# The T half of a triangular inverse kept in its PSUM bank, in a fused delta-rule attention and mixture kernel

## The reference, cut to what matters

```python
def step(S, inp):
    qt, kt, vt, gt, bt = inp
    S = S * jnp.exp(gt)[..., None]
    err = jnp.einsum('bhk,bhkv->bhv', kt, S)
    delta = bt[..., None] * (vt - err)
    S = S + kt[..., None] * delta[:, :, None, :]
    ot = jnp.einsum('bhk,bhkv->bhv', qt, S)
    return (S, ot)
```

## Time and profile before

| | us |
|---|---|
| median of 3 runs | 5753.49 (5748.64 to 5756.43) |
| the profiled execution, its own time | 5752.94 |
| its span | 5751.1 |
| PE busy | 5436.6 (95%) |
| DVE busy | 4370.1 (76%) |
| ACT busy | 3026.7 (53%) |
| POOL busy | 1729.5 (30%) |

### The profile page before, as it was taken

The page is one execution under the profiler, slowest core; times in us unless marked ns, Lnnn a source line. Parts: engine busy times, 40 slices in busy tenths (PEclk is TensorE's granted clock), DMA queues, the critical chain, the costliest instruction groups (busy, mean ns, idle before and its releaser), DMA issues. The chain is left out here.

```text
span 5751.1 us, 87343 instructions
## 1 busy us (share of the span) xinstructions
PE 5436.6 (95%) x28996; PEld 3760.2 (65%) x28996; DVE 4370.1 (76%) x9309; ACT 3026.7 (53%) x5708; POOL 1729.5 (30%) x1766
## 2 busy tenths in 40 slices
PE   5599999999999999999999999999999999799999
PEld 2277777777777777777777777777777777444444
DVE  6688888888888888888888888888888888121110
ACT  3366666666666666666666666666666665100110
POOL 2233333333333333333333333333333333000000
PEclk8799999999999999999999999999999999899999
DMA  2111111111111111111111111111111110331221
GB/s 77 47 28 38 30 38 30 36 30 36 30 35 30 37 30 38 30 38 30 38 30 38 30 34 34 30 38 30 37 30 38 30 30 19 106 112 51 71 75 50
DMA packets 192038, 235.69 MB, mean 41 GB/s; under 512 B 41576, under 2 KB 136424, under 8 KB 187504
## 3 DMA queue, kind: packets, MB, share of 16 engines
q1 hardware_dynamic: 111016, 188.22, 10.9%
q10 hardware_dynamic: 80584, 41.95, 2.5%
HBM read 183.75 MB, written 46.38 MB: 40 GB/s over the span
## 5 line engine op out<-in xcount | busy, mean ns | idle before, releaser
L713 PE MATMUL bank<-xT,weights 128*128 128x512 f32 x4096 | 2128.4, 607 | 32.9 <-PEq L155 32.9
L1451 POOL TENSOR_TENSOR KR<-KR,decay_u 128x256 f32<-128x256 f32 x768 | 635.3, 827 | 1599.1 <-PE bank L733 1591.1
L733 PEld LDWEIGHTS bank<-KQ,KR 128*128 128x128 f32 x7168 | 915.3, 191 | 267.9 <-issue 241.6
L1035 DVE TENSOR_TENSOR KQ<-KQ,decay_u 128x512 f32<-128x512 f32 x896 | 789.5, 881 | 284.3 <-PE bank L733 279.2
L733 PE MATMUL bank<-KQ,KR 128*128 128x128 f32 x7168 | 963.3, 277 | 18.2 <-DVE KQ L1035 17.3
L1020 DVE SCALAR_TENSOR_TENSOR conv<-pre,taps,conv 128x512 f32<-128x512 f32 x1152 | 938.5, 815 | 18.2 <-ACT conv L1243 8.5
L1051 DVE COPY_PREDICATED all_pairs<-level_mask,bank 128x256 f32<-128x256 int32 x1792 | 822.4, 523 | 0.0
L713 PEld LDWEIGHTS bank<-xT,weights 128*128 128x128 f32 x4096 | 664.4, 192 | 186.5 <-issue 164.5
L757 PEld LDWEIGHTS bank<-T_inv,pairs 128*128 128x128 f32 x1536 | 270.9, 190 | 566.1 <-ACT T_inv L1308 326.0
L757 PE MATMUL bank<-T_inv,pairs 128*128 128x128 f32 x1536 | 495.6, 407 | 113.1 <-ACT T_inv L1308 112.9
L1308 ACT ACTIVATE T_inv<-bank 128x256 fp32r<-128x256 f32 x640 | 247.1, 386 | 479.6 <-PE bank L775 476.4
(11 more groups left out here) (185 smaller groups left out, 8805.7 us busy)
## 6 DMA issues: line engine op xcount, KB each, us to landing
decay_u<-decay_scratch SPq DMA_DIRECT2D x128, 510.0 KB
beta_u<-beta_scratch SPq DMA_DIRECT2D x128, 256.0 KB
y_in<-y_scratch SPq DMA_DIRECT2D x32, 1024.0 KB, 4.8
y_scratch<-y_rn ACTq DMA_DIRECT2D x112, 256.0 KB, 2.3
xt<-in_L_attn_hidden_states SPq DMA_DIRECT2D x8, 1024.0 KB, 5.4
x_in<-in_L_attn_hidden_states SPq DMA_DIRECT2D x28, 256.0 KB, 5.0
out<-o_out ACTq DMA_DIRECT2D x28, 256.0 KB, 2.0
w<-in_L_ffn_W SPq DMA_DIRECT2D x8, 704.0 KB, 4.8
```

The source lines that it names most:

```text
L713: last = nc.tensor.matmul(bank[w % 2][:], weights[par][:, w, k, :], xT[:, k, u % J * UC:(u % J + 1) * UC], start=k == 0, stop=k == KC - 1)
L733: last = nc.tensor.matmul(to[:, :, i], KR[:, cols(i)], second if i < COUPLES else second[:, :, ::-1, ::-1], start=True, stop=True)
L1035: nc.vector.tensor_tensor(second_halves, second_halves, pair[:, :, 0:1].unsqueeze(1).to_broadcast([P, 2, blocks, 1 << l]), ALU.mult).then_ ...
L1451: nc.gpsimd.tensor_tensor(firsts, firsts, second.to_broadcast([P, 2, UC >> (l + 2), 1 << l]), ALU.mult).then_inc(keys_scaled.sem, 1)
```

## The change

T of the inverse is no longer rewritten from a fresh product at each level. It stays in PSUM bank 5, and each level adds to it: one matmul for each couple, with a gathered weight tile XX (POOL copies the parts of X into it, three copies for a level) and a plain copy of Z as the moving operand (ACT, `keep_z`, five more copies). So `inverse_xt(l)` splits into `inverse_t(l)`, two matmuls of 128 columns for levels 1 to 5, and `inverse_x(l)`, two matmuls. The first T comes from the first X by two matmuls of 256 columns with a swap matrix, and ACT copies it (`take_t(m, 0)`), so `first_inverse` on DVE goes. Z moves from bank 5 to the upper half of bank 2, beside X. The pair products are in natural order, so `keep_pairs` copies with one instruction instead of two, and ACT turns the kept pairs with three copies instead of one. The blocks of X are stored with the turned sequences first. The lists of calls on PE, ACT, DVE and POOL are rearranged.

```diff
@@ PE: the first T, Z, T and X
-            def transpose_pairs():
-                wait(pe, pairs_ready, m, 1)
-                for i in range(B):
-                    last = nc.tensor.matmul(bank[5][:, cols(i)], pairs_first[:, cols(i)], ident_r[:], start=True, stop=True)
+            def first_t():
+                wait(pe, x1_ready, m, 1)
+                for turned in range(2):
+                    last = nc.tensor.matmul(bank[5][:, to], swap_r[:], swapped, start=turned == 0, stop=turned == 1, ...)
             def inverse_z(l):
-                if l == 1:
-                    wait(pe, t1_ready, b, 1)
-                else:
-                    wait(pe, t_ready, b, l - 1)
+                wait(pe, t_ready, b, l)
+                if l >= 2:
+                    wait(pe, x_ready, b, l - 1)
-            def inverse_xt(l):
+            def inverse_t(l):
+                wait(pe, z_kept, b, l)
+                wait(pe, xx_ready, b, l)
+                for r in range(COUPLES):
+                    last = nc.tensor.matmul(firsts_in_place(bank[5], l, r), XX[:, cols(r)], Z[:, cols(r)],
+                                            start=False, stop=True, skip_group_check=True)
+                last.then_inc(t_done.sem, 1)
+            def inverse_x(l):
-                if l < LEVELS - 1:
-                    for i in range(B):
-                        last = nc.tensor.matmul(bank[5][:, half_cols(i)], X[b % 2][:, cols(i)],
-                                                halves(ZI[:, cols(i % COUPLES)], l, i // COUPLES), start=True, stop=True)
@@ DVE
             def add_identity_to_z(l):
-                wait(dve, z_done, b, l)
+                if l < LEVELS - 1:
+                    wait(dve, z_kept, b, l)
+                else:
+                    wait(dve, z_done, b, l)
-            first_inverse()
@@ ACT
+            def keep_z(l):
+                wait(act, z_done, b, l)
+                nc.scalar.activation(Z[:], bank[2][:, UC // 2:UC], ACT.Copy).then_inc(z_kept.sem, 1)
             silu_v()
-            take_t(1)
+            keep_z(1)
+            store_output()
+            take_t(b, 1)
             take_x(1)
-            store_output()
+            keep_z(2)
             take_projection(2)
...
+            take_t(m, 0)
             take_projection(1)
@@ POOL
+        def gather_x(u, l, before):
+            wait_apart(pool, x_ready.sem, x_ready.at(u, l - 1), pool_waits_passed)
+            wait_apart(pool, t_done.sem, t_done.at(u, l), pool_waits_passed)
...
+            nc.gpsimd.tensor_copy(halves(XX[:], l, 1), halves(natural, l, 1).bitcast(F32))
+            for i in range(COUPLES, B):
+                last = nc.gpsimd.tensor_copy(halves(XX[:, cols(couple(i))], l, 0),
+                                             halves(X[u % 2][:, cols(in_x(i))], l, 0).bitcast(F32))
+            last.then_inc(xx_ready.sem, 1)
```

More of the change, by code:

```diff
@@ L579, in attention, with couple, sides, all_first_sides @@
     COUPLES = B // 2
-    def in_order(ap, i):
-        return ap if i < COUPLES else ap[:, ::-1]
-    def first_sides(tile, l, r):
+    def couple(i):
+        return min(i, B - 1 - i)
+    def sides(tile, l, first, step, start, blocks):
+        size = 1 << l
+        ap = tile[:]
+        return bass.AP(tensor=ap.tensor, offset=ap.offset + first * P + start,
+                       ap=[list(ap.ap[0]), [step * P + size - 2 * start, 2], [2 * size, blocks], [1, size]])
+    def first_sides(tile, l, r):
+        return sides(tile, l, r, B - 1 - 2 * r, 0, P >> (l + 1))
+    def all_first_sides(tile, l):
+        return sides(tile, l, 0, COUPLES, 0, COUPLES * P >> (l + 1))
+    def in_x(i):
+        return (i + COUPLES) % B
+    def x_second_sides(tile, l, r):
+        size = 1 << l
+        natural, turned = in_x(r) * P + size, in_x(B - 1 - r) * P
+        ap = tile[:]
+        return bass.AP(tensor=ap.tensor, offset=ap.offset + natural,
+                       ap=[list(ap.ap[0]), [turned - natural, 2], [2 * size, P // (2 * size)], [1, size]])
+    def all_x_second_sides(tile, l):
+        return sides(tile, l, 0, COUPLES, 0, COUPLES * P >> (l + 1))
+    def firsts_in_place(tile, l, r):
         size = 1 << l
@@ L800, in apply_inverse @@
                 for i in range(B):
-                    last = nc.tensor.matmul(bank[7][:, cols(i)], X[u % 2][:, cols(i)], to[:, cols(i)], start=True, stop=True)
+                    last = nc.tensor.matmul(bank[7][:, cols(i)], X[u % 2][:, cols(in_x(i))], to[:, cols(i)], start=True, stop=True)
                 return last
@@ L913, in step @@
             level(0)
-            inverse_xt(1)
+            inverse_t(1)
             refine(c, 1)
+            inverse_x(1)
+            inverse_z(2)
             project(2, (3,))
-            inverse_z(2)
             level(1)
+            inverse_t(2)
+            correct_by_residual(1)
+            inverse_x(2)
             project(3, (0,))
-            inverse_xt(2)
-            correct_by_residual(1)
+            inverse_z(3)
             project(3, (1,))
-            inverse_z(3)
+            level(2)
+            inverse_t(3)
+            output()
+            inverse_x(3)
+            inverse_z(4)
             project(3, (2,))
-            level(2)
-            inverse_xt(3)
-            output()
+            level(3)
+            inverse_t(4)
+            next_state()
+            inverse_x(4)
             project(3, (3,))
-            inverse_z(4)
-            next_state()
-            level(3)
-            inverse_xt(4)
+            inverse_z(5)
             project(0, (0,))
-            inverse_z(5)
+            level(4)
+            inverse_t(5)
+            right_side()
+            inverse_x(5)
             project(0, (1,))
-            level(4)
-            inverse_xt(5)
+            inverse_z(6)
             project(0, (2,))
-            inverse_z(6)
-            right_side()
             level(5)
-            inverse_xt(6)
+            inverse_x(6)
             project(0, (3,))
@@ L1475, in step @@
                 squares_left(s.a, 1)
+                for l in range(2, LEVELS - 1):
+                    gather_x(s.b, l, None)
                 return
```

150 lines of the change are left out of this document (87 added, 63 removed).

## The result

The changed kernel takes 6727.15 us, median of 4 runs (6722.37 to 6728.86), beside 5751.07 for the kernel before (also 4 runs). The ratio is 1.1692, 95% interval [1.1678, 1.1706]. The forecast was 6360 us with a range to 6530: the direction held, the size did not. The profiled execution took 6722.37 us, its span is 6720.6.

The account below looks back on a forecast made before the run. The prediction took PE to bound the kernel, busy 35.28 of a 36.14 us step. It added 3.9 of lateness and 1.0 of low clock, 4.9 us over about 124 steps, 608 us on 5752.9: 6360 us, range 6080 to 6530.

Parts of the forecast that it names:

- the main term: Level 1 T and X copies queue behind ACT's output store; PE waits 3.1 us at `inverse_z(2)`, `level(1)` ends 3.85 late.
- PE stays the bound: Rival: with y_rn early enough PE sees only its lighter work, 2.2 us a step less, 5480 us; faster, chance 0.06.
- the idle: PE's waits in a step: 1.3 us at `inverse_t(1)`, 3.1 at `inverse_z(2)`, 0.6 at `inverse_z(4)`, 1.7 at `right_side`.
- the clock term: PE's clock falls to half rate after the new idle; 3.4 us at half rate costs up to 1.7, taken as 1.0.
- the sum of 3.9: `level(5)` and all after it late by 1.75 at `right_side` plus 2.16 of work formerly done earlier: 3.9 us a step.
- DVE's chain to the state: From `scale(1)` to the new state on DVE, 13.4 us, nearly all busy; starting at 2133.3, state at about 2146.9.
- `right_side`: PE waits 1.7 us there for DVE's state and starts 1.75 us later than before.
- the small edits: POOL's three gathers at most 1.5 us and hidden; `first_inverse` goes where DVE idles anyway; reversed operands cost nothing.
- the 1.3 us of PE's work: PE's saving a step from fewer T matmuls: 1.1 us on five levels and 0.2 on the first T.
- the clock falls in every step and the gathers collide: Rival: 3.9 + 1.7 + 0.5 = 6.1 us a step, 6510 us; chance 0.14.
- DVE is not last at `right_side`: Rival: only PE's own lateness counts, 2.7 us a step without a clock fall, 335 us, 6090; chance 0.14.

Follow-up runs that it names:

- The store's edit: Changed kernel with the store of the output moved behind the copies of T and X of level 1 on ACT: 6268.67 us, ratio 1.0897.
- the same swap in the old kernel: Kernel before, with its store of the output put ahead of the copies of T and X of level 1 on ACT: 5936.3 us, ratio 1.0313.
- The fillers: Changed kernel with five unread 512-column matmuls a step in PE's three idle gaps, no wait removed: 6352.78 us, ratio 1.1043.
- The experiment that moved it: Changed kernel with `right_side` put back behind Z of level 6 and two quarters of the projection on PE: 6665.6 us, ratio 1.1584.
- all orders mended: Changed kernel with store and `right_side` late, ACT's Z, T, X copies ahead of work waiting for DVE, Z of levels 2 and 4 behind a projection quarter: 5666.24 us, 0.9847.
- both edits: Changed kernel with the store behind T and X of level 1 and `right_side` behind Z of level 6: 6269.16 us, ratio 1.0898.
- T and X of level 5 moved too: Changed kernel with store and `right_side` late, plus ACT's copies of T and X of level 5 ahead of `silu_squares(1)`: 5932.54 us, ratio 1.0317.

## Why the prediction was right, and where it failed

**Right: the chain.** The step called the main term, T and X behind the store, is there as forecast: from `scale(0)` to the store 2.89 us (2948.75 to 2951.64) where 2.88 was taken, and 2.83 of wait where 3.1 was taken. The store's edit alone gave back 458 us, and the same swap in the old kernel cost 181. What the rival "PE stays the bound" needed, an early y_rn, did not arise.

**Right in size, in part by luck: the idle.** 6.73 us of waits in the step shown, against 6.7 forecast. The two waits at the head are each 0.3 shorter than forecast as the rows count them, and the one for the state 0.66 longer, so misses cancel in the sum.

**Failed, first and most: the clock term.** The prediction took 1.0 us a step, with "a stretch of 3.4 us at half rate costs up to 1.7" as the bound. The fillers measure 2.93. The step that failed is the count of stretches: the bound priced one of 3.4 us in a step, as the earlier trace rows show after one wait. Two waits, 0.97 and 2.83 with 1.6 us of work between them, go with 6.83 us at half rate (81 such stretches in 91 steps), and a further stretch of 3.41 comes in about every second step, mostly behind the 2.36 of `right_side`: 7.8 us in the mean. The conversion was right in kind, about 0.38 us lost for each us at half rate (2.93 / 7.8). It is under the half, and some of the slow time is spent waiting: 0.90 of the 6.83 in the step shown. The 1.93 missing are 245 us of the 367 by which the forecast was low.

**Failed, second: the sum of 3.9.** At full clock the step is 4.64 longer, 0.74 more than forecast, 94 us. (The other 28 of the 367 are 3 more steps than the 124 counted, and the time outside the steps.) Most of it comes out at `right_side`, which waited 2.36 and not 1.7. The term that was mis-sized is DVE's chain to the state. The walk put 13.6 us from the start of `scale(1)` to the new state on DVE. In the kernel with all gaps filled it takes 14.44 (2980.91 to 2995.35):

```profile
2980.91 0.70 DVE L1089 TENSOR_TENSOR KQ<-KQ,decay_u 128x512 f32<-128x512 f32 x1 [0.32 <-PE bank L758]
...
2987.43 0.42 DVE L1134 TENSOR_TENSOR ZI<-bank,ident_each 128x256 fp32r<-128x256 f32 x1 [0.32 <-ACT Z L1362]
...
2992.07 0.42 DVE L1134 TENSOR_TENSOR ZI<-bank,ident_each 128x256 fp32r<-128x256 f32 x1 [0.92 <-ACT Z L1362]
...
2994.24 1.11 DVE L1171 SCALAR_TENSOR_TENSOR state<-state,chunk_decay,bank 128x128 f32<-128x128 f32 x4
```

I had counted this chain as nearly all busy. In the kernel before it is, with one wait of 0.20:

```profile
2141.37 0.42 DVE L1079 TENSOR_TENSOR ZI<-bank,ident_each 128x256 fp32r<-128x256 f32 x1 [0.20 <-PE bank L757]
```

Now DVE idles in it 0.32 for Z of level 4 and 0.92 for Z of level 5, which ACT has to copy first, and another 0.32 just ahead of `scale(1)`. `keep_z` lies between PE and DVE on levels 1 to 5; I had priced that only at level 1.

**Wrong in its reason: `right_side`.** That it would wait for the state held. But the prediction read this as the only thing late there. The experiment that moved it found X of level 5 nearly as late (2.07 against 2.36), behind `silu_squares(1)`. The queue of ACT was read at the head of the step and not at its middle, where the same pattern stands.

**Right: the small edits.** POOL's three copies were taken as at most 1.5 us and hidden. Their rows, in the line's view of the kernel after (ns, least, median, most), are

```profile
L1542 POOL CAST XX<-X x1280: 226/236/749, 270.3 to 5859.6; 128x64 fp32r<-128x64 f32 x183
...
L1540 POOL CAST XX<-X x640: 279/291/764, 270.0 to 5859.2; 128x128 fp32r<-128x128 f32 x160
```

so 0.76 for three by the medians, and the page of the kernel after gives Z, and not XX, as what ended every wait of `inverse_t` (idle before it, us, and what ended it):

```profile
L800 PE MATMUL bank<-Z,XX 128*128 128x128 f32 x1280 | 299.1, 319 | 125.1 <-ACT Z L1349 125.1
```

Of the 1.3 us of PE's work some 0.9 to 1.05 is found: 0.90 in the kernel with all orders mended, and 35.18 - (40.83 - 6.70) = 1.05 in the one with the fillers. The rule of the Trainium skill that was weighed, page "TensorE: Matmul & The Clock Gate", section "Back-to-back issue gap", states the gap of an isolated matmul, and by it the T matmuls would have saved nothing. The measured saving is nearer to the rows.

Of the rivals, "the clock falls in every step and the gathers collide", 6510, was right on the first, and still 217 short of the result, as it too counted one stretch of 3.4 us in a step; what the gathers cost DVE was not measured apart. "DVE is not last at `right_side`" fell with the wait of 2.36 for the state.

## What to carry to other kernels

When an engine's list is rearranged, walk every place where a copy that PE needs stands behind an instruction that waits for a third engine, and not only the first: a wait that is covered by another shows nothing in the profile until the other is gone, so removals are to be tested together as well as one by one. New idle time in a walk that ran at full clock is to be priced twice, as idle and as slow stretches behind it, and not with one stretch a step as the bound: here 5.7 us of new idle a step brought 7.8 us at half rate and 2.93 of loss. A change that saves matmuls on the bounding engine can be right and lose all the same by the order it came with; changing the order here turned 17% slower into 1.5% faster.

## What the runs showed of the hardware that I had not expected

With two waits close together, 0.97 and 2.83 us, the clock stood at 0.50 for 6.83 us, 81 times in 91 steps, twice the stretch of the earlier trace rows. Nor does it take one wait as long as 2.83, in the same 4000 us of the other kernels: with both edits no wait of PE is over 2.07 us, and its 100 steps have 69 stretches of 3.41 us at half rate; with T and X of level 5 moved too, no wait is over 1.3 us and its 107 steps have 22. Filling the gaps with unread matmuls made the kernel 374 us faster with no wait removed, and filling only the 2.83 one gave 332 of these. A similar amount of idle (4.2 and 4.6 us a step) went with 0.5 and with 2.5 us at half rate in two kernels, so the total of idle doesn't tell the clock. And the accumulating matmuls with a gathered tile cost no more than plain ones: two of them take 0.25 us in the kernel with the fillers (2980.63 to 2980.88), as two plain ones of Z do (L790, 2982.50 to 2982.75):

```profile
2980.63 0.42 PE L800 MATMUL bank<-Z,XX 128*128 128x128 f32 x2
2980.88 0.61 PE L837 MATMUL bank<-U_r,X 128*128 128x128 f32 x4
```
